# Cross attention of a decoder on one Trainium2 core: unmasked periods dealt anew, starts reordered, PE given fill matmuls

## The reference

```python
q, k, v = heads(x @ Wq.T + bq), heads(ctx @ Wk.T + bk), heads(ctx @ Wv.T + bv)
scores = einsum('bhqd,bhkd->bhqk', q, k) / 4      # layer 0: where(mask == 0, -1e9, scores)
out = einsum('bhqk,bhkd->bhqd', softmax(scores), v) @ Wo.T + bo
```

## Time and profile before

| | us |
|---|---|
| median of 3 runs | 2820.03 (2814.89 to 2820.06) |
| profiled execution, its own time | 2802.67 |
| its span | 2800.7 |
| PE busy | 2412.1 (86%) |
| DVE busy | 1942.9 (69%) |
| ACT / POOL busy | 1122.3 / 1029.3 |
| masked cross attention, first instruction to the first of the next stage | 466.8 to 956.3 |
| unmasked cross attention, first instruction to the first of the next stage | 2101.0 to 2596.2 |

### The profile page before, as it was taken

How to read it: one execution, slowest core, us unless ns; L and a number is a source line. 1 busy time by engine, 2 the same in 40 slices (tenths; PEclk the granted TensorE clock), 3 DMA queues, 4 the chain that set the end, 5 groups by cost and what they waited for, 6 DMA issues and landing times. The chain is left out here.

```text
span 2800.7 us, 50704 instructions
## 1 busy us (share of the span) xinstructions
PE 2412.1 (86%) x17441; PEld 2031.8 (73%) x17442; DVE 1942.9 (69%) x5156; ACT 1122.3 (40%) x2057; POOL 1029.3 (37%) x1419
## 2 busy tenths in 40 slices
PE   3999996899999699999999999987887998885870
PEld 3778885566665489999999999986764666663860
DVE  6999992567677456656767666657673787885558
ACT  2655663455555322222222222212563655552650
POOL 3545552111111064316725335111111344545664
PEclk7999998799999799999999999998997998986885
DMA  3243101323321210012212212004003334220535
GB/s 98 99 136 117 52 1 31 80 65 111 80 65 45 76 40 30 30 46 93 70 34 71 70 34 75 29 26 149 8 1 84 92 105 112 79 55 3 154 132 235
DMA packets 163949, 203.94 MB, mean 73 GB/s; under 512 B 21027, under 2 KB 138062, under 8 KB 163792
## 3 DMA queue, kind: packets, MB, share of 16 engines
q1 hardware_dynamic: 132704, 152.04, 18.4%
q10 hardware_dynamic: 15440, 26.22, 2.6%
q0 software_dynamic: 15648, 23.70, 2.5%
HBM read 95.49 MB, written 75.45 MB: 61 GB/s over the span
## 5 line engine op out<-in xcount | busy, mean ns | idle before, releaser
L1629 PE MATMUL m_gu<-m_x_hi,m_w_hi 128*128 128x256 f32 x1632 | 461.2, 283 | 17.8 <-issue 10.4
L1629 PE MATMUL m_gu<-m_x_hi,m_w_lo 128*128 128x256 f32 x1632 | 456.6, 280 | 0.0
L1629 PE MATMUL m_gu<-m_x_lo,m_w_hi 128*128 128x256 f32 x1632 | 456.5, 280 | 0.0
L1666 ACT ACTIVATE m_sg<-m_gu 128x256 f32<-128x256 f32 x408 | 157.1, 385 | 661.0 <-PE m_gu L1629 661.0
L1138 ACT ACTIVATE x_pt<-x_ps 128x1024 f32<-128x1024 f32 x256 | 262.3, 1025 | 223.5 <-PE x_ps L966 221.9
L1702 DVE TENSOR_TENSOR m_h<-m_sg,m_gu 128x256 f32<-128x256 f32 x408 | 171.5, 420 | 250.9 <-ACT m_sg L1666 248.3
L1629 PEld LDWEIGHTS m_gu<-m_x_hi,m_w_hi 128*128 128x128 f32 x1632 | 310.3, 190 | 21.7 <-issue 11.8
L1629 PEld LDWEIGHTS m_gu<-m_x_lo,m_w_hi 128*128 128x128 f32 x1632 | 308.4, 189 | 0.0
L1629 PEld LDWEIGHTS m_gu<-m_x_hi,m_w_lo 128*128 128x128 f32 x1632 | 308.3, 189 | 0.0
L1240 DVE CUSTOM_DVE_ANT_0 x_ps<-x_ps,x_mb 128x256 f32<-128x256 f32 x512 | 201.4, 455 | 116.2 <-PE x_ps L966 116.1
L1618 PE MATMUL m_yp<-m_w_hi,m_h_hi 128*128 128x256 f32 x816 | 238.5, 292 | 4.8 <-DVE m_h_lo L1704 4.5
(11 more groups left out here) (324 smaller groups left out, 5592.7 us busy)
## 6 DMA issues: line engine op xcount, KB each, us to landing
yt<-zero SPq DMA_DIRECT2D x8, 2048.0 KB, 10.7
x_qpack<-x_qh SPq DMA_DIRECT2D x128, 128.0 KB, 3.0
x_kpack<-x_kh SPq DMA_DIRECT2D x128, 128.0 KB, 3.1
m_yr<-yt SPq DMA_DIRECT2D x16, 1024.0 KB, 13.6
m_x<-xs SPq DMA_DIRECT2D x36, 258.0 KB
xs<-zero SPq DMA_DIRECT2D x8, 1072.0 KB, 6.1
m_x<-xs SPq DMA_DIRECT2D x32, 268.0 KB
c_cx<-in_ctx SPq DMA_DIRECT2D x32, 256.0 KB, 3.1
```

Source lines behind the costliest of these rows:

```text
L1629: ins = pe.matmul(gu[:, m % 4, n, :], wp[n][:, c, m * P:m * P + P], xp_[:, c, :], start=(c == 0 and k == 0), stop=(c == KC - 1 and k == 2))
L1666: act.activation(sg[:, m % 4, :], gu[:, m % 4, 0, :], ACT.Silu).then_inc(silu_ready, 1)
```

## The change

Six edits, all in `xattn_stage`.

1. **Banks of the first sequence.** `proj(what, n)` gives each projection of sequence 0 a PSUM bank of its own (`FIRST_BANK`), later ones still `bank(PROJ)`.
2. **Start.** Before the periods PE runs `turn_in(0)`, `project_keys(0)`, `project_queries(0)`, `project_values(0)` (before: queries, keys, values, each behind ACT's reading of the last). ACT now turns the key weights and DVE the query weights, with a semaphore each. SP packs keys before queries, POOL does `low_keys(0)` and `low_queries(0)` behind its first memset. The other engines skip period -1.
3. **Fill.** In query period 0 of both stages PE issues bfloat16 products of 512 columns whose results nobody reads: 12 before `query_scores(0, 0)`, and 4 before each of four others (masked) or of three (unmasked).
4. **Unmasked order.** PE, ACT and DVE have an `open_period` beside the old order, which stays as `masked_period`. `place` becomes `take_places` and `place_rows`; `one_hot` becomes `mark_chosen` and `count_chosen`, the second a period later, so `rank` is a period later as well; `choose` gives up its first three operations to `affinities`; the last two statistics operations of `add_output` become `spread_of_rows`.
5. **POOL unmasked.** `rstd_of` first and a period later; `add_bias`, `low_queries` and `low_keys` each get one more wait, on `hit_ready`, `gates_ready` and `experts_picked`, that is on DVE's piece before maximum 0, 2 and 5; `low_keys` waits for query scores 5 in place of 4.
6. **Scatter.** `slots_out` issues two DMAs a call, four calls a sequence, two between any two other pieces or pairs of pieces; the second block of a sequence goes out a period later, and there is one more period (`range(-1, B + 5)`).

The masked stage keeps its order in the periods, and gets edits 1 to 3.

```diff
         KEY, QUERY, WEIGH, PROJ, OUT, ROUTE = 0, 2, 4, 5, 6, 7
+        FIRST_BANK = (OUT, ROUTE, PROJ, WEIGH)
+        def proj(what, n):
+            return bank(PROJ if n else FIRST_BANK[what])
...
-        PERIODS = range(-1, B + 4)
+        PERIODS = range(-1, B + 5)
...
-            for p in PERIODS:
+            pack_keys(0)
+            pack_queries(0)
+            load_context(1)
+            for p in PERIODS[1:]:
...
                 beside_maximum(n - 1, 2)
+                if not masked and n >= 5:
+                    pool.wait_ge(gates_ready, n - 4)
                 pool.tensor_tensor(ql[:], qf[:], qh[:].bitcast(F32), ALU.subtract).then_inc(ql_ready, 1)
...
-                beside_maximum(n - 1, 4)
+                beside_maximum(n - 1, 4 if masked else 5)
+                if not masked and n >= 4:
+                    pool.wait_ge(picked, n - 3)
                 pool.tensor_tensor(kl[:], kf[:], kh[:].bitcast(F32), ALU.subtract).then_inc(kl_ready, 1)
...
-                beside_maximum(n + 2, 5)
+                beside_maximum(n + 2, 5 if masked else 0)
+                if not masked and n >= 2:
+                    pool.wait_ge(hit_ready, n - 1)
...
-                for j in range(topk):
+                for j in range(first, first + 2):
...
+                if u == 0:
+                    low_keys(0)
+                    low_queries(0)
...
+            def fill(n, products):
+                if n == 0:
+                    for _ in range(products):
+                        pe.matmul(ps[:, KEY, :], st.identb[:], st.identb[:].unsqueeze(1).to_broadcast([P, 4, P]),
+                                  start=True, stop=True)
...
-            for p in PERIODS:
+            turn_in(0)
+            project_keys(0)
+            project_queries(0)
+            project_values(0)
+            def masked_period(p):
...
                 at(l, key_scores, 7)
+                fill(q, 12)
                 at(q, query_scores, 0)
...
+            def spread_of_rows(n):
+                u = n % U
+                s.after(s.n)
+                dve.bn_aggr(var[:, u, 0, :], stats[:, u, 0, :])
+                dve.bn_aggr(var[:, u, 1, :], stats[:, u, 1, :]).then_inc(varr, 1)
...
+            def open_period(p):
+                a, q, l, r = p + 1, p, p - 2, p - 3
+                at(l - 1, spread_of_rows)
+                at(r - 1, count_chosen)
+                at(q, maxima, 0)
```

244 lines of the change are left out of this document (184 added, 60 removed).

## The result

| | median us | runs, us |
|---|---|---|
| before | 2818.95 | 7 runs, 2812.6 to 2821.9 |
| changed | 2801.21 | 7 runs, 2800.0 to 2811.8 |

The ratio is 0.9957, 95% interval 0.9942 to 0.9972: faster by 0.43%, some 12 us by the ratio and 18 by the medians. The forecast was 2767 us, range 2750 to 2795. The sign was right, the size was not: a quarter to a third of the 52.5 us came.

A forecast was written before the change was run, and what follows sets the result against it. Masked attention was taken as PE-bound, the unmasked one as losing time to waits and half clock above PE's 21.7 us a period. Savings summed to 52.5 us, giving 2767 us against the 2820.0 median, range 2750 to 2795.

The forecast's parts named there:

- nine full periods: Unmasked periods with DVE's and POOL's full load: 23.1 us each at full clock, 5.5 extra for the expert load; 25.7 us saved.
- last query period, drain, tail: End of the unmasked stage: more even stretches may keep the clock, 3.6 us saved; final 20 scatters unchanged, 0.
- the sum of waits: PE's remaining waits in a full unmasked period: 0.3, 0.3, 0.2 and 0.6 us, 1.4 above PE's 21.7.
- the first rival: Full unmasked periods: clock still falls, six of nine openings cold, fill useless for the clock; 2785 us, chance 0.17.
- the 1.5 us of stall: Each full unmasked period: small DVE operations held up by large POOL operations; placing those beside maxima removes 1.5 us.
- The offset that I carried over: Whole kernel: profiled execution 2802.7 us against median 2820.0, a difference taken as unchanged by the change.
- the prediction's own signs of being wrong: Periods over 24.5 us, cold openings in most, a DMA wait heading every period, or a drain longer than before.
- Query period 1: Second query period of each stage: starts warm in place of cold; 2.5 us saved unmasked, 2.0 masked.
- Lighter periods: Four unmasked periods before the full ones: to about 21.0, 22.4, 23.0 and 23.0 us; 5.3 us saved.
- Starts: Stage starts: first scores earlier by 1.2 us unmasked, 3.2 masked; query period 0 with fill saves 4.5 us each.
- The slower rival: Unmasked periods: packed keys come late, PE waits at every period's head and opens cold; 2828 us, chance 0.05.
- a lock of GpSimd's descriptor writing: Scatters beside `weigh_experts` and `place_rows`: certain DVE operations would lock GpSimd out and lengthen them; slack expected, no size given.

The follow-up runs named there:

- again_before: The kernel before, unchanged, profiled again beside others on one chip: 2791.3 us, one run.
- again_after: The changed kernel, unchanged, profiled a second time: 2772.8 us, one run, where the kernel before took 2797.6 us.
- after_timed: The changed kernel, unchanged, timed against the kernel before: 2767.0 us, ratio 0.9889.
- after_third: The changed kernel, unchanged, timed once more against the kernel before: 2763.1 us, ratio 0.9883.
- before_third: The kernel before, unchanged, profiled again on a chip where signals came late: 2810.1 us, one run.
- the first profile of the changed kernel: The profiled execution of the changed kernel that belongs to the result, with late signals: 2801.21 us.
- sets 2 and 5: Two groups of runs, each on one chip beside its own kernel before, which took 2795.5 and 2796.5 us; no late signals in number.
- fours: Changed kernel with scatters in fours, all of one sequence in one period, none at the period's opening; timed ratios 0.9896 and 0.9920.
- fours_timed: Changed kernel with scatters in fours of one sequence a period, timed against the kernel before: 2766.1 us, ratio 0.9896.
- scatter_fours: Changed kernel with scatters in fours of one sequence a period, none at the opening, first run: 2758.7 us, one run.
- scatter_last: Changed kernel with all 128 scatters of the unmasked stage moved behind its last period: 2895.8 us, one run.
- new_unmasked: Changed kernel with the masked stage's code put back to that of the kernel before: 2774.4 us, ratio 0.9928.
- best: Changed kernel with scatters in fours, experts' weights loaded in quarters, and 12 unused products in each query period 1 and the last query period: 2780.6 us, ratio 0.9899.
- no_fill: Changed kernel without the unused products of query period 0 in both stages: 2807.2 us, ratio 0.9985.
- no_beside: Changed kernel without the waits holding POOL's three large unmasked operations beside maxima 0, 2 and 5: 2798.9 us, one run.
- fours_again: Changed kernel with scatters in fours of one sequence a period, timed where signals came late: 2788.5 us, ratio 0.9920.
- sets 3 and 4: Two groups of runs, both on chip 13, beside a kernel before of 2812.1 and 2814.3 us; signals late with scatters in the periods.
- sets 1, 2 and 5: Three groups of runs on chips 9, 4 and 12, beside a kernel before of 2795.5 to 2797.6 us; no late signals in number.

## Why the prediction missed, point by point

The traces without late signals show the steps undisturbed: again_before against the three traces of the changed kernel (again_after, after_timed, after_third). The last column is the same with late signals, the kind of the result: before_third against the first profile of the changed kernel. Lengths between the marks, us:

| step | predicted | before | changed | saved | saved, signals late |
|---|---|---|---|---|---|
| masked start to first scores | 3.2 | 19.7 | 18.2 to 18.6 | 1.3 | 1.5 |
| query period 0, masked | 4.5 | 24.1 | 20.2 to 20.4 | 3.8 | 3.1 |
| query period 1, masked | 2.0 | 27.4 | 27.5 | 0 | 0 |
| unmasked start to first scores | 1.2 | 19.5 | 18.3 to 18.7 | 1.1 | 0.2 |
| query period 0, unmasked | 4.5 | 21.0 | 18.6 to 21.7 | 0.8 | 1.1 |
| query period 1, unmasked | 2.5 | 25.0 | 24.9 to 26.4 | -0.5 | 0 |
| four lighter periods | 5.3 | 94.8 | 92.2 to 95.4 | 1.0 | 5.1 |
| nine full periods | 25.7 | 238.6 | 212.8 to 217.5 | 24.0 | 1.9 |
| last query period, drain, tail | 3.6 | 91.4 | 99.0 to 99.8 | -7.9 | -3.2 |
| second mixture of experts | 0 | 115.1 | 114.8 to 119.1 | -2.6 | 0.1 |

The column of the undisturbed traces takes the mean of the three. It adds up to 21.0 us; the spans are 18.3 to 20.4 us apart, the rest lies between the stages. The timed medians of sets 2 and 5 are 28.5 and 33.4 us apart: the trace of the kernel before (2791.3 us) was one of its shortest runs, those of after_timed and after_third the longest of their four. Even undisturbed, 31.5 us of the 52.5 are missing by the traces and 19 to 24 by the medians. The last column adds up to 9.7 us, with spans 9.0 us apart, near the 12 to 18 us of the result. Of what is missing there, 23.8 us are the nine full periods (240.1 to 238.2 us, one trace each).

- **Nine full periods: this is the step that failed in the result.** Without late signals the even order does what the walk said: 23.1 us, the clock at 1.00 and 5.5 us for the load (28.6) in again_after. Two things of the step were wrong. The first is the sum of waits, 1.4 us: it has 0.3 us for the exponential before key scores 1, and no term for a signal that comes late beside a scatter. In the first profile that wait was 0.84 to 0.90 us in each of ten periods, behind the pair of scatters that the change puts at the period's opening. The second is "PE would be busy 94% of the period, and the row of 93% had clock 1.00, so I take the full clock". In the first profile the clock fell once in each of these ten periods, and even undisturbed it fell in four of the nine of after_third. So the first rival had the mechanism, down to one of its four waits, though not what lengthens it, and its time, 2785, was nearer. Its price of 2.1 us for a fall was about right: a fall alone made a period of after_third 1.5 or 3.2 us longer. Too low was the number of periods, six of nine, and it had nothing for the idle time itself; together the ten periods took 3.4 us more than 23.1 each. And the 1.5 us of stall were a gain of the undisturbed kind only, as before_third shows.
- **The offset that I carried over.** I took the profiled execution's 2802.7 us as 2820.0 less a constant. It was of the kind without late signals, the timed runs of the other. The 17 us gap was the one sign of it, and I explained nothing by it. Also, two of the prediction's own signs of being wrong came: periods over 24.5 us and a drain longer than before. A profiled execution below all timed runs by more than their spread has to be taken as another condition.
- **Last query period and drain: wrong sign.** I gave 3.6 us for a clock that lasts and 0 for the tail. The period fell to either clock (20.7 to 26.5 us). The tail is not "20 again": from the last `rstd` to the first expert product 33.0 us became 34.4, since half of each sequence's scatters is a period later; in fours it is 32.5. The other 4.8 us lie between `nmT` 15 and that `rstd` (34.1 to 38.9 us; 34.5 in fours_timed, whose clock lasted through the period before). That is the clock rather than the order: scatter_fours is the program of fours_timed and took 38.8 us with the clock already low, and scatter_last, without scatters there, has both lengths too (33.8 and 38.1). With the pairs, new_unmasked came to this stretch at full clock, lost it there and took 39.9. In the first pair of profiles 14.1 us had been gained at `nmT` 14; 0.9 went in the last query period, 7.7 in the drain and 4.3 in the second mixture of experts (114.9 to 119.2 us), so the spans are 1.2 us apart.
- **Query period 1: wrong.** "Starts warm in place of cold" was true and paid nothing in the traces compared; the period waits for its first exponentials, and the clock falls there. In five others with the same masked code the masked one took 23.8 to 26.4 us, so it falls to either clock as well. The warm products of best didn't change that.
- **Lighter periods: mis-sized** undisturbed, 5.3 for 1.0 (5.1 where signals are late, as two of the four took 27.9 and 28.1 us before). Two reach 23.0 us, but the first pays for the clock (24.6 and 26.2 in two traces, 23.0 in the third, 21.8 before).
- **Starts.** The fill's gain was right within 1 us for each stage where measured against no_fill, one trace; the unmasked row of the table has 0.8, within what that period varies by itself. The 3.2 us of the masked start were the distance to one trace: 20.7 us to the first scores in the earlier trace rows, 19.7 and 19.8 in the two later traces of the kernel before.
- **The slower rival** (keys late at the head of every period) appeared at no period but that of the load.

The prediction weighed a lock of GpSimd's descriptor writing, from the Trainium skill, SBUF — State Buffer, section SBUF: two separate sides, against the pairs. A scatter took 0.97 to 1.03 us in nearly all rows with the pairs as without, so no run here shows that lock lengthening one.

The second mixture of experts is a cost that I didn't look for: code that the change leaves alone, and 4.0 us more in two of the three traces. VectorE's smallest operation there, the destinations, meets a GpSimd scatter or misses it, for the whole loop. Where it meets one it ends with it: in again_after 0.48 us from 2601.76, beside a scatter from 2601.27 to 2602.25. The form's row in again_after, then in scatter_fours:

```profile
L2488 DVE TENSOR_SCALAR m_dest<-m_spot 128x4 uint32<-128x4 f32 x15 | 7.2, 481 | 0.5
```

```profile
L2488 DVE TENSOR_SCALAR m_dest<-m_spot 128x4 uint32<-128x4 f32 x16 | 2.7, 170 | 0.6
```

Both modes occur with one program (fours: 115.2 and 119.4 us), and with the kernel before too (the operation takes 170 ns in again_before, 453 in before_third), so it is chance and no price of the change; a queue order that settles it would be worth 4 us.

## What to carry over

Compare the profiled execution with the timed runs before summing anything: a gap beyond their spread says that the trace and the time belong to different conditions, and a forecast needs one case for each. Where one engine's order has no slack left, a scatter beside the signals that its next wait hangs on can decide the whole gain. Moving the scatters away from the period's opening, as the fours do, took 1.3 to 1.9 us off each period where signals were late. Four of nine full periods of after_third lost the full clock without a wait ahead of it, so a sum that takes it for every period is a best case. A single run of a kernel whose starts and drain fall to either clock can be 10 us off; the sum of steps must be made over stretches that repeat.

## What the runs showed of the hardware

- Signals between engines can come 0.4 to 2.6 us late while GpSimd issues an indirect DMA, between a fifth (20 of 90 in no_beside) and somewhat over half (64 of 116 in fours_again) of TensorE's signals beside scatters in sets 3 and 4, none in sets 1, 2 and 5. The kernel before takes 16 to 24 us more there, the changed one 34 to 38 (2801 against 2763 to 2767).
- The fall to half clock in the first profile's periods stood each time behind 0.84 to 0.90 us of idle time before key scores 1. That idle time was not needed for a fall (four of the nine full periods of after_third fell without it), and as much of it elsewhere did not bring one: in fours_again TensorE idles 1.1 to 1.2 us before query scores 0 in most periods, and the clock falls in three of eleven. A fall made an otherwise equal period 1.5 or 3.2 us longer (24.6 and 26.3 us against 23.1 in after_third). The Trainium skill, TensorE: Matmul & The Clock Gate, section Part 1: The HAM clock gate, says that activity releases the throttle. The traces agree: with the fill the clock was 0.81 instead of 0.57 in the unmasked query period 0, and with the warm products 0.88 instead of 0.81 in the masked query period 1. Time followed in the first case only (20.4 against 23.9 us, but 28.2 against 27.4).
- Two engines that share a loop can fall into one of two steady phases, 6.8 or 7.1 us for three tiles here, and stay in it for the whole stage: the destinations took 169 to 170 ns on average in eleven of the twenty traces and 441 to 471 in the other nine.
